# Where the products of the last block's first half are summed in a Mamba and mixture-of-experts kernel

## The reference

```python
def step(h, ts):
    dt_t, B_t, C_t, u_t = ts
    dA = jnp.exp(dt_t[..., None] * A)
    h = h * dA + (dt_t * u_t)[..., None] * B_t[:, None, :]
    y = jnp.einsum('bds,bs->bd', h, C_t)
    return (h, y)
...
y = ys.transpose(1, 0, 2) + xc * D
y = y * jax.nn.silu(z)
return y @ out_proj_w.T
```

## Time and profile before

| what | value |
|---|---|
| median of 3 runs | 1489.9 us (1487.7 to 1492.16) |
| the profiled execution, its own time | 1492.3 us |
| its span, first to last instruction | 1490.5 us |
| mean granted TensorE clock | 0.923 of full speed |
| TensorE busy with products | 1241.0 us (83%) |
| VectorE busy | 1243.3 us (83%) |
| GpSimd busy | 1203.2 us (81%) |
| ScalarE busy | 896.3 us (60%) |

### The profile page before, as it was taken

One profiled execution on the slowest core, in us unless ns is written; L12 is line 12 of the kernel. 1 busy time (PEld: TensorE's weight loads), 2 busy tenths in 40 slices (PEclk: granted clock), 3 DMA queues, 4 the chain that ended last, 5 costly groups with the idle time before them and its releaser, 6 DMA issues.

```text
span 1490.5 us, 17206 instructions
## 1 busy us (share of the span) xinstructions
PE 1241.0 (83%) x4966; PEld 906.0 (61%) x4966; DVE 1243.3 (83%) x1547; ACT 896.3 (60%) x1972; POOL 1203.2 (81%) x638
## 2 busy tenths in 40 slices
PE   3765575789979998989998997999998998889977
PEld 2542121577667756767676766876776676646556
DVE  6589875799978998799988997899989988978744
ACT  3543434586756856676766765776767574645432
POOL 0435888898898879888899889998999899987740
PEclk8567877899999999999999999999999999979989
DMA  5674454678586757877598858876788678456640
GB/s 174 228 254 147 157 203 137 241 240 268 168 312 215 236 162 238 280 230 254 161 323 248 242 168 268 281 238 206 239 309 254 189 224 309 153 196 214 220 130 29
DMA packets 131518, 325.79 MB, mean 219 GB/s; under 512 B 15176, under 2 KB 29904, under 8 KB 120928
## 3 DMA queue, kind: packets, MB, share of 16 engines
q1 hardware_dynamic: 112224, 272.91, 54.0%
q0 software_dynamic: 13056, 41.95, 12.2%
q10 hardware_dynamic: 6144, 9.83, 1.8%
HBM read 259.75 MB, written 39.71 MB: 201 GB/s over the span
## 4 chain that ended last, share of the span: by engine, by line
POOL 27%; issue 24%; PE 20%; DVE 11%; ACT 5%; DMA 2%; SPq 0%; DVEq 0%; POOLq 0%; ACTq 0%
PE prod L1036 15%; POOL hxc L762 11%; POOL dbu L751 9%; DVE state L1423 7%; POOL slot_x L738 4%; DMA late<-moe 2%; PE prod L1088 2%; PE prod L1223 2%; PE prod L1224 1%; POOL hxc L770 1%; DVE hxc L1391 1%; ACT state L838 1%; DVE prod L1436 1%; POOL dtu L790 1%; DVE late L1488 1%
## 5 line engine op out<-in xcount | busy, mean ns | idle before, releaser
L1423 DVE TENSOR_TENSOR_SCAN state<-state,carry,dbu 128x512 f32<-128x512 f32 x512 | 657.7, 1285 | 120.1 <-ACT state L838 64.7
L751 POOL TENSOR_TENSOR dbu<-dtu,bb 128x1024 f32<-128x1024 f32 x256 | 631.3, 2472 | 36.8 <-DVE state L1423 35.2
L762 POOL TENSOR_TENSOR hxc<-hxc 128x1024 f32<-128x1024 f32 x155 | 377.6, 2436 | 97.3 <-DVE hxc L1391 97.1
L838 ACT ACTIVATE state<-dt,par 128x512 f32<-128x512 f32 x512 | 352.7, 692 | 54.5 <-DVE hxc L1391 39.1
L1391 DVE TENSOR_TENSOR hxc<-state,cb 128x512 f32<-128x512 f32 x512 | 353.9, 691 | 37.3
L1036 PE MATMUL prod<-late 128*128 128x256 f32 x1136 | 268.6, 394 | 46.4 <-DMA late<-moe 24.6
L1036 PE MATMUL prod<-xsT,late 128*128 128x256 f32 (+1 forms) x1280 | 266.3, 363 | 27.7 <-issue 20.3
L1036 PEld LDWEIGHTS prod<-late 128*128 128x128 f32 x1136 | 227.2, 203 | 83.8 <-issue 56.0
L1036 PEld LDWEIGHTS prod<-xsT,late 128*128 128x128 f32 x1280 | 223.7, 193 | 74.7 <-issue 40.5
L1088 PE MATMUL prod<-hxc,ident 128*128 128x512 f32 x212 | 120.6, 702 | 63.1 <-DVE hxc L1391 48.1
L836 ACT COPY carry<-state 128x1 f32<-128x1 f32 x384 | 60.8, 158 | 158.1 <-DVE hxc L1391 145.3
(11 more groups left out here) (168 smaller groups left out, 1250.2 us busy)
## 6 DMA issues: line engine op xcount, KB each, us to landing
bb<-bc_rows SPq DMA_DIRECT2D x256, 256.0 KB
cb<-bc_rows SPq DMA_DIRECT2D x256, 256.0 KB
late<-moe SPq DMA_DIRECT2D x40, 1028.0 KB, 5.4
late<-moe SPq DMA_DIRECT2D x40, 1024.0 KB, 7.0
hxc<-hxc POOLq DMA_DIRECT2D x36, 512.0 KB, 8.0
slot_x<-xc SPq DMA_DIRECT2D x18, 512.0 KB, 5.1
xs<-slot_x SPq DMA_DIRECT2D x31, 256.0 KB, 5.4
slot_y<-ys ACTq DMA_DIRECT2D x31, 256.0 KB, 5.4
```

The lines of the kernel that those rows point to most:

```text
L751: nc.gpsimd.tensor_tensor(dbu[:, v % 3, :, :], dtu[:, n % 2, 2 * h:2 * h + 2, :], b, ALU.mult).then_inc(dbu_ready, 1)
L762: nc.gpsimd.tensor_tensor(hxc[:, to, :, :], hxc[:, to, :, :], hxc[:, piece, :, :], ALU.add).then_inc(summed, 1)
L838: nc.scalar.activation(state[:, k % STATES, :], dt[:, (2 * n + h) % 3, k % 2, :], ACT.Exp, scale=par[:, P_ALOG + col(k):P_ALOG + col(k) + ...
L1423: nc.vector.tensor_tensor_scan(state[:, k % STATES, :], state[:, k % STATES, :], dbu[:, v % 3, c, :], carry[:, n % 2, col(k):col(k) + 1], ...
```

## The change

The first half of block 7 is summed as blocks 1 to 6 are: one chain of four groups of four. Before, it had three groups of four and four single products, each given to TensorE. The second half stays as it was (two groups of two and twelve single products). `events()` now asks for each half whether it is whole, where it asked whether the block lay between the first and the last.

```diff
-GROUPS = [(ALONE * NS,) * 2] + [(((4, 4, 4, 4),),) * 2] * (NB - 2) + [(((4,),) * 3 + ALONE * 4, ((2,),) * 2 + ALONE * 12)]
+GROUPS = [(ALONE * NS,) * 2] + [(((4, 4, 4, 4),),) * 2] * (NB - 2) + [(((4, 4, 4, 4),), ((2,),) * 2 + ALONE * 12)]
...
     for n in range(NB):
-        if 0 < n < NB - 1:
-            for h in range(2):
+        whole = [Y_CHAIN[Y_UNIT[(2 * n + h) * NS][0]][0] in WHOLE for h in range(2)]
+        for h in range(2):
+            if whole[h]:
                 out[n * BASE_STEP + DU_AT + 32 * h].append(("C", "DU%d" % h, n))
                 out[n * BASE_STEP + DU_LINK + 32 * h].append(("Y", "DLINK", 2 * n + h))
         for name, at in STEPS_C.items():
-            if 0 < n < NB - 1 and name[:2] == "YE":
+            if name[:2] == "YE" and whole[int(name[2]) // 2]:
                 continue
```

## The result

The changed kernel took 1521.66 us in the median (1520.15 to 1522.96, 4 runs), the one before 1491.03 us beside it: a ratio of 1.0191, 95% interval 1.0158 to 1.0224 (23.6 to 33.4 us; here as below the ratio is an estimate of its own and can differ a little from the quotient of the two medians). The forecast was 1501.0 us (1494 to 1506). The sign was right. The size was not, and the time lies outside the range.

The account below looks back on a forecast made before the run. The prediction took GpSimd's place in its list at the eighth gather to set the time in the changed half. GpSimd's added 8.60 us plus 2.5 us of landing, 11.1 us on 1489.9, gave 1501.0 us (range 1494 to 1506).

Parts of the forecast that it names:

- TensorE loses: Block 7's first half, ahead of the eighth gather: seven ACCs, about 13.8 us of work, go from covered time; taken as 0.
- After the gather: From MX0 to the end TensorE's work keeps its order with 0.85 us of slack, so everything moves by 11.1 us.
- GpSimd ahead of the first gather: DLINK and first LINK, 1.70 us, absorbed by idle time; second LINK, with no idle behind it, costs 0.85 us.
- The three adds and the third `LINK`: GpSimd's list before the eighth gather: adds of units 13 to 15 cost 6.90 us, the LINK 0.85.
- The landing: The eighth gather, queued right behind the third LINK, lands 2.5 us later, bounded between 0 and 6.0.
- The gather passes the LINK: Rival at the eighth gather's landing: no extra landing time, 8.60 us alone, 1498.5 us; chance 0.20.
- the full price of the queue: Rival: third LINK lands as late as the slowest, the eighth gather behind it: 8.60 + 6.0 = 14.6 us, 1504.5; chance 0.17.
- Given back by the clock: Rival: TensorE's clock is up from MX0's start, returning 7.1 of 11.1 us: 1493.9 us, within 0.3%; chance 0.11.
- Relief of TensorE: Last rival: fewer ACCs before the experts' last tile let the first gather leave 5.4 us earlier, 1484.5 us; chance 0.05.

Follow-up runs that it names:

- plan kept: The changed kernel with a phantom cost of 4 counted at the four steps that lost ACCs, so every experts' piece keeps its step of before: 1503.64 us.
- loads later: The kernel before with only SP's loads for block 1 of the output stage six steps later: 1492.59 us.
- the two dense ones: The kernel before with block 0's gathers three to a step and SP's loads for block 1 six steps later (1500.64 us) or at step 468 (1495.05 us).
- the fifth: The kernel before with one group of four fewer in block 7's first half, experts' pieces kept in place, SP's loads for block 1 six steps later: 1492.48 us.
- the four other spacings: The kernel before with phantom cost -4, -1, +1 or +4 at each of four steps, moving only experts' pieces and banks: 1519.21, 1506.88, 1499.83, 1508.59 us.
- the kernels with `LATER`: ScalarE's experts' pieces held back two steps instead of one, on the kernel before (1526.33 us) and on plan alone (1531.23 us).
- plan alone: The kernel before, operations untouched, with 4 less counted at four steps, so the experts' pieces stand where the change puts them: 1519.21 us.
- the adds behind the gathers: The changed kernel with experts' pieces kept in place and the last three adds and last LINK of the half moved behind block 0's gathers: 1502.64 us.
- the last run but one: The kernel before with block 0's gathers three to a step and SP's loads for block 1 at step 468: 1495.05 us.
- the last run: The changed kernel with experts' pieces kept in place, block 0's gathers three to a step and SP's loads for block 1 at step 468: 1500.53 us.

## Why the prediction was wrong

**The step that failed** is the one under "TensorE loses": "They only lengthen an idle of 6.38 us. I take nothing for them." It priced the seven `ACC`s as work, and for work that was right. It did not ask what else counts them. `cost()` gives each 4, and `events()` spaces the experts' pieces over all steps by the sum. Of the 30.6 us some 18 come from this (1521.66 against 1503.64 with the plan kept; 1.0191 against 1.0068), which the prediction put at 0. The same mistake stands in "After the gather": "in the same order" was said of the last stretch, where it holds (167.2 us against 166.7), and tacitly taken for everything before it, where it does not.

**The terms, by the run with the plan kept.** GpSimd ahead of the first gather (`DLINK` and two `LINK`s) was put at 0.85 us and measured 1306.40 - 1304.60 = 1.80. The first gather scatters by more than that: from 1299.51 to 1305.72 in the five kernels without these operations, from 1304.95 to 1307.83 in the four with them (places kept in all). The means are 1303.4 and 1306.6, so the term can be as large as 3 us and isn't known to 1 us.

The three adds and the third `LINK` up to the eighth gather were put at 7.75 us; first to eighth gather take 23.58 us instead of 15.77, so 7.81. The landing was put at 2.5 us more and measured 5.19 - 3.37 = 1.82. The sum in the two traces is 11.4 us against 11.1, and the kernel measured 11.9 us above the one before. The mechanism holds. That the sums agree to 0.3 us is in part luck: a term 1 us too small and one 0.7 too large cancel, and the interval of the measurement is 6 to 14 us.

The rule of the Trainium skill that the forecast drew on (page "DMA: Bandwidth & Descriptors", section "Two DMAs through the same engine are not ordered": descriptors within one queue of one DMA engine start in order) asks for more than 0, and the two traces with a gather right behind a `LINK` agree with 5.19 and 5.20 us. While these gathers were out the software queue moved 0.79 MB and took 65.4 and 67.3% of sixteen engines (0.29 MB and 27.6% in the kernel before). But a landing depends on SP's queue too: with no `LINK` ahead it took 3.3 to 4.5 us where SP's queue moved 0.35 to 0.94 MB, and 5.0 once where the software queue itself moved 0.53 MB. The two with a `LINK` had 0.33 and 0.30 MB beside them, so the nearest partner is the kernel with the loads later (3.27 us, 0.35 MB), and the `LINK` costs some 1.9 us.

**The rivals.** "The gather passes the LINK" (0 more) and "the full price of the queue" (6.0 more) both fall to the same landing. "Given back by the clock" falls: the mix ran 14.23 us at 0.50, as before. "Relief of TensorE" did not come, and more, no gain at this place showed in the time as the kernel stands: five kernels with an earlier eighth gather or less of GpSimd's work took between 0.999 and 1.0048 of the time before. Two were held back by the loads beside the gather, the two dense ones without these loads by block 1's gathers, and the fifth had its eighth gather hardly earlier.

**What the new spacing does** is shown in part. Shown: it alone costs 27.5 us with no operation changed; about 20 of these remain with the weights' loads cut; each of the four other spacings, in either direction, costs 7 to 28 us, and VectorE's idle time and its waits for ScalarE grow with it. The chain TensorE, ScalarE, VectorE is read from one place, and the kernels with `LATER` changed neither cured it nor pinned it down further. Not separated are the places of the pieces from their new PSUM banks, and the waits from TensorE's lower clock; which of the 256 moved pieces cost the most was not measured.

**The parts don't add.** 27.5 and 11.9 us make 39.4, and the change costs 30.6. By the ratios it is 2.4% against 1.9%, and their intervals together are wider than the gap. In the traces the first gather of plan alone comes at 1329.68 and that of the change at 1323.62, 6.1 us earlier. The forecast's last rival would give 5.4 us for the dropped `ACC`s; but 3.5 us of the difference are there at step 448 already (1254.50 against 1250.97), ahead of any dropped `ACC`. How much is relief and how much the scatter between executions stays open.

## What to carry to other kernels

Before an operation is priced as work, look for everything that counts it: a planner's cost sum, a buffer table, a due time. Here removing four `ACC`s from the last block moved 256 other pieces over the whole kernel. When a change touches a generator of orders, compare the two orders engine by engine before forecasting, and if only a local change is wanted, pin the rest (one phantom cost gave 18 us back).

And where a wait is relieved, look up when the next operation of the same kind is ready: a gain of 4 and of 10 us at block 0's mix was gone by that of block 2 (1377.84 and 1374.70, against 1374.67 before), through a wait and the half clock at block 1's.

## What was not expected of the hardware

The time in which a 128 KB gather landed followed what SP's queue moved meanwhile: 2.8 us beside 0.06 MB or less, 3.3 to 4.2 beside 0.35 to 0.61 MB, 4.1 to 4.5 beside 0.78 to 0.94 MB, and 6.3 to 6.4 us beside 1.49 to 1.60 MB. Right behind a 512 KB accumulating DMA of the same queue, with 0.30 to 0.33 MB of SP's, it was 5.2.

TensorE's clock: after waits as short as 2.13 us (with the adds behind the gathers) and 2.46 us (the last run but one) before block 1's mix, the granted clock over the next 16 and 18.4 us was 0.57 and 0.63, near its level of 1.2 GHz; where the same mix began without a wait, it stayed at the full 2.4 GHz (1.00 from 1353 to 1369 us of the kernel before). In the two runs where `MX0` of block 0 waited only 1.19 us, it stayed at full speed too, and so it did after the 1.57 us before block 1's mix of the last run. In that run a wait of 2.78 us, at 1352.94, was followed by four products with the identity in 3.03 us instead of 1.88, and the clock was full again at 1359.91. So a short wait can cost more than itself: four products of the mix take 2.08 us instead of 1.13.

The scatter of one kernel is larger than the first three runs showed: the kernel before gave 1486.4 to 1503.2 us over 23 runs, about 1.1%. A 0.3% difference between two medians of three, which the forecast took for the limit, is within that.
